# Row blocks in the middle of the next tile's products, and products in couples on halves of TensorE's rows

## The reference, cut to what matters

```python
Kf = jnp.einsum('bjd,ed->bje', F, K_w)
S = jnp.einsum('bid,bjd->bij', F, Kf)
out = jnp.einsum('bij,ijd->bid', S, W)
out = out + jnp.einsum('bid,ed->bie', F, Q_w)
```

## Time and profile before

| what | value |
|---|---|
| median of three runs | 606.97 us |
| the profiled execution | 606.42 us |
| its span, first to last instruction | 604.6 us |
| TensorE busy (matmuls) | 596.4 us, 99% |
| VectorE busy | 399.2 us, 66% |
| ScalarE busy | 401.5 us, 66% |
| mean granted clock of TensorE | 0.998 of full speed |

### The profile page before, as it was taken

The page is one execution under the profiler, slowest core; times in us unless marked ns, Lnnn a source line. Parts: engine busy times, 40 slices in busy tenths (PEclk is TensorE's granted clock), DMA queues, the critical chain, the costliest instruction groups (busy, mean ns, idle before and its releaser), DMA issues.

```text
span 604.6 us, 17904 instructions
## 1 busy us (share of the span) xinstructions
PE 596.4 (99%) x7690; PEld 526.3 (87%) x7690; DVE 399.2 (66%) x412; ACT 401.5 (66%) x696; POOL 0.2 (0%) x4
## 2 busy tenths in 40 slices
PE   9999999999999999999999999999999999999995
PEld 7888989889898898988989898898988989889895
DVE  6556768567685675947749475685756768567486
ACT  7888393874938659295692947939387493865920
POOL 0000000000000000000000000000000000000000
PEclk9999999999999999999999999999999999999999
DMA  8644847457575575755657566484754857557177
GB/s 338 262 141 160 330 165 282 183 185 305 191 281 172 210 266 208 279 196 210 242 192 287 203 238 249 143 319 174 277 209 173 318 179 284 173 209 273 70 281 279
DMA packets 29452, 138.12 MB, mean 228 GB/s; under 512 B 3264, under 2 KB 3776, under 8 KB 21312
## 3 DMA queue, kind: packets, MB, share of 16 engines
q1 hardware_dynamic: 20736, 75.83, 31.8%
q10 hardware_dynamic: 8640, 61.15, 28.4%
HBM read 69.86 MB, written 67.11 MB: 227 GB/s over the span
## 4 chain that ended last, share of the span: by engine, by line
PE 98%; DVE 1%; issue 1%; DVEq 0%
PE ps L509 20%; PE ps L447 20%; PE ps L449 19%; PE ps L448 19%; PE ps L541 18%; DVE o_sb L372 1%; PE ps L576 1%; DVEq L49 0%; DVE o_sb L382 0%; PE ps L467 0%; PE ps L465 0%; PE ps L469 0%; DVE f_hi L388 0%; DVEq L115 0%
## 5 line engine op out<-in xcount | busy, mean ns | idle before, releaser
L337 DVE TENSOR_TENSOR f_lo<-f_ring,f_hi 128x1024 fp32r<-128x1024 f32 x124 | 151.8, 1224 | 168.2 <-ACT f_hi L217 166.6
L231 ACT ACTIVATE q_out<-ps 128x512 f32<-128x512 f32 x256 | 156.9, 613 | 6.6 <-PE ps L449 0.2
L222 ACT ACTIVATE kf<-ps 128x512 f32<-128x512 f32 x256 | 155.8, 609 | 3.5
L372 DVE TENSOR_TENSOR o_sb<-ps,q_out 128x1024 f32<-128x1024 f32 x127 | 145.1, 1215 | 19.4 <-PE ps L541 19.3
L240 ACT ACTIVATE s_t<-ps 128x512 f32<-128x512 f32 x32 | 19.1, 598 | 175.8 <-PE ps L509 175.8
L509 PE MATMUL ps<-f_ring,kf 128*64 128x64 f32 x4096 | 123.5, 222 | 0.3 <-issue 0.3
L509 PEld LDWEIGHTS ps<-f_ring,kf 128*64 128x64 f32 x4096 | 121.1, 138 | 2.6 <-issue 0.8
L541 PEld LDWEIGHTS ps<-s_t,w_sb 64*128 64x128 f32 x2048 | 115.6, 188 | 5.6 <-issue 5.6
L541 PE MATMUL ps<-s_t,w_sb 64*128 64x128 f32 x2048 | 118.6, 274 | 0.0
L447 PE MATMUL ps<-f_hi,k_hi 128*128 128x512 f32 x255 | 101.0, 396 | 0.0
L447 PE MATMUL ps<-f_hi,q_hi 128*128 128x512 f32 x256 | 100.0, 391 | 0.0
(11 more groups left out here) (39 smaller groups left out, 160.3 us busy)
## 6 DMA issues: line engine op xcount, KB each, us to landing
out<-o_sb SPq DMA_DIRECT2D x127, 512.0 KB, 3.5
f_ring<-f_t ACTq DMA_DIRECT2D x58, 1024.0 KB, 4.8
f_ring<-f_t SPq DMA_DIRECT2D x4, 1024.0 KB, 10.6
f_ring<-f SPq DMA_DIRECT2D x8, 256.0 KB, 5.3
w_sb<-w SPq DMA_DIRECT2D x1, 2048.0 KB, 17.8
out<-o_sb SPq DMA_DIRECT2D x2, 256.0 KB, 2.6
o_sb<-first SPq DMA_DIRECT2D x1, 192.0 KB, 2.9
o_sb<-first ACTq DMA_DIRECT2D x1, 192.0 KB, 3.4
```

The source lines that it names most:

```text
L222: nc.scalar.activation(kf[:, c // 2, c % 2 * CK:(c % 2 + 1) * CK, :, :].rearrange("d k h i -> d (k h i)"), ps[:, 2 * c % 8, :], COPY).then ...
L231: nc.scalar.activation(q_out[:, t % 2, :, :].rearrange("d i (h b) -> d i h b", h=2)[:, :, :, at:at + CK], q_bank(t * CHUNKS + c).rearrange ...
L337: nc.vector.tensor_tensor(f_lo[:, v % SPLIT, :], f_unit(v), f_hi[:, v % SPLIT, :].bitcast(F32), ALU.subtract).then_inc(flo_done, 1)
L372: nc.vector.tensor_tensor(o_sb[:, n % OBUF, :, :, :].rearrange("d x s b -> d s x b"), ps[:, bank:bank + 2, :].rearrange("d s (x b) -> d s ...
```

## The change

- The row blocks of tile t no longer follow the products of tile t+1; they stand in their middle, after the products of chunk 7 (MID = 8). The scores of tile t+1 follow the products of chunk 15 directly.
- From tile 1 on, a chunk's two products (each three matmuls of 128 rows) are cut at row 64 into six couples. `first_halves` issues three couples: the Q product on rows 0 to 63 beside the K product on rows 64 to 127. `second_halves` issues the other three: the K product on rows 0 to 63 beside the Q product on rows 64 to 127, added to the same banks. The second halves of a chunk come after the first halves of the next one, and wait for their own first halves (`half_done`). So TensorE's order is, with f and s for first and second halves: f0 f1 s0 f2 s1 f3 s2 f4 s3 f5 s4 f6 s5 f7 s6 s7, row blocks 0 to 7 of the tile before, f8 f9 s8 f10 s9 f11 s10 f12 s11 f13 s12 f14 s13 f15 s14 s15, then the scores.
- VectorE adds the row blocks between `both_f(v + 6)` and `low_f(v + 7)`.
- Waits follow: the first four row blocks wait for the copies of chunks 4 to 7, f8 to f11 wait for the sums of blocks 4 to 7, the scores wait for the copies of the last chunks, and the splits wait for `k_done` as well as `q_done`.
- The waits on `zeros_done` between products (FILL) are gone.

```diff
-FILL = {1: 0, 2: 56}
-FILL.update((t, 108) for t in range(3, TILES - 1))
-FILL[TILES - 1] = 132
+MID = 8
...
                 both_f(v + 4)
                 low_f(v + 5)
                 both_f(v + 6)
+                for k in range(UNITS):
+                    sum_out(t, k)
                 low_f(v + 7)
                 both_f(v + 8)
                 low_f(v + 9)
-                for k in range(UNITS):
-                    sum_out(t, k)
...
+            def products(step):
+                if step < TILES * CHUNKS - LATE:
+                    return (q_of(step), q_done), (k_of(step), k_done)
+                return (k_of(step), k_done), (k_of(step + 1), k_done)
...
+            def passes(dst, w_hi, w_lo, c, rows, first):
+                hi = f_hi[rows, c // 2 % SPLIT, piece_cols(c)]
+                lo = f_lo[rows, c // 2 % SPLIT, piece_cols(c)]
+                yield nc.tensor.matmul(dst, w_hi[rows, :], hi, start=first, stop=False)
+                yield nc.tensor.matmul(dst, w_hi[rows, :], lo, start=False, stop=False)
+                yield nc.tensor.matmul(dst, w_lo[rows, :], hi, start=False, stop=not first)
+
+            def first_halves(step):
+                (a, _), (b, _) = products(step)
+                for ins_a, ins_b in zip(passes(*a, lower, True), passes(*b, upper, True)):
+                    pass
+                ins_a.then_inc(half_done, 1)
+                ins_b.then_inc(half_done, 1)
+
+            def second_halves(step):
+
+                pe.wait_ge(half_done, 2 * (step - CHUNKS + 1))
+                (a, a_sem), (b, b_sem) = products(step)
+                for ins_b, ins_a in zip(passes(*b, lower, False), passes(*a, upper, False)):
+                    pass
+                ins_b.then_inc(b_sem, 1)
+                ins_a.then_inc(a_sem, 1)
...
-                    elif e % 2 == 0:
-
-
-                        pe.wait_ge(out_done, (t - 1) * UNITS + 5 + e // 2)
+
+                    pe.wait_ge(kf_copied, t * CHUNKS + max(2 * e + 2, 13 + e // 2))
+                    if e % 2:
+                        pe.wait_ge(q_copied, min(t * CHUNKS + 13 + e // 2, TILES * CHUNKS - LATE))
...
-                        pe.wait_ge(kf_copied, (t + 1) * CHUNKS + 13 + k)
-                        pe.wait_ge(q_copied, min((t + 1) * CHUNKS + 13 + k, TILES * CHUNKS - LATE))
+                        pe.wait_ge(kf_copied, (t + 1) * CHUNKS + MID - 3 + k)
+                        pe.wait_ge(q_copied, (t + 1) * CHUNKS + MID - 3 + k)
...
+                    if t >= 1 and MID <= c < MID + 4:
+
+                        pe.wait_ge(out_done, (t - 1) * UNITS + 5 + c - MID)
...
+                    first_halves(n)
+
+                    if c >= 1 and c != MID:
+                        second_halves(n - 1)
+                    if c == MID - 1:
+                        second_halves(n)
+                        rows_tile(t - 1)
+                if t >= 1:
+                    second_halves(min((t + 1) * CHUNKS - 1, TILES * CHUNKS - LATE))
...
             for t in range(TILES):
                 scores_tile(t)
                 if t < TILES - 1:
+
                     project(t + 1)
-                rows_tile(t)
+            rows_tile(TILES - 1)
```

More of the change, by code:

```diff
@@ L97, in build @@
         fhi_done, flo_done = sem("fhi_done"), sem("flo_done")
+        half_done = sem("half_done")
         k_done, kf_copied = sem("k_done"), sem("kf_copied")
@@ L208, in split_first @@
                 wait(act, q_done, 2 * (c // 2 - SPLIT) + 2)
+                wait(act, k_done, 2 * (c // 2 - SPLIT) + 2)
                 nc.scalar.activation(f_hi[:, c // 2 % SPLIT, piece_cols(c)], f_cols(c), COPY).then_inc(fhi_first, 1)
@@ L216, in split_f @@
                 act.wait_ge(q_done, 2 * (v - SPLIT) + 2)
+                act.wait_ge(k_done, 2 * (v - SPLIT) + 2)
                 nc.scalar.activation(f_hi[:, v % SPLIT, :], f_unit(v), COPY).then_inc(fhi_done, 1)
             def copy_kf(t, c):
-                act.wait_ge(k_done, t * CHUNKS + c + 1)
+                n = t * CHUNKS + c
+                act.wait_ge(k_done, n + 1 if n < TILES * CHUNKS - LATE else TILES * CHUNKS)
                 nc.scalar.activation(kf[:, c // 2, c % 2 * CK:(c % 2 + 1) * CK, :, :].rearrange("d k h i -> d (k h i)"),
@@ L225, in copy_q @@
             def copy_q(t, c):
-                act.wait_ge(q_done, t * CHUNKS + c + 1)
+                n = t * CHUNKS + c
+                act.wait_ge(q_done, n + 1 if n < TILES * CHUNKS - LATE else TILES * CHUNKS)
                 if c == 0:
@@ L328, in both_first @@
                 wait(dve, q_done, 2 * (c // 2 - SPLIT) + 2)
+                wait(dve, k_done, 2 * (c // 2 - SPLIT) + 2)
                 if c == 4:
@@ L350, in both_f @@
                 dve.wait_ge(q_done, 2 * (v - SPLIT) + 2)
+                dve.wait_ge(k_done, 2 * (v - SPLIT) + 2)
                 nc.vector.tensor_copy(f_hi[:, v % SPLIT, :], f_unit(v)).then_inc(fhi_dve, 1)
@@ L449, in three, with k_of, q_of @@
                 return nc.tensor.matmul(dst, w_lo[:, :], hi, start=False, stop=True)
+            def products(step):
+                if step < TILES * CHUNKS - LATE:
+                    return (q_of(step), q_done), (k_of(step), k_done)
+                return (k_of(step), k_done), (k_of(step + 1), k_done)
+            def k_of(c):
+                return ps[:, 2 * c % 8, :], k_hi, k_lo, c
+            def q_of(c):
+                return q_bank(c), q_hi, q_lo, c
+            def passes(dst, w_hi, w_lo, c, rows, first):
[17 more added lines that the diff above has]
+                ins_a.then_inc(a_sem, 1)
             def k_product(c):
@@ L470, in k_halves @@
                 ins.then_inc(k_done, 1)
[L472 to L498, removed]
             def scores(t, e):
@@ L514, in scores_tile @@
                 for e in range(UNITS):
[L515 to L522, removed]
-                    elif e % 2 == 0:
-                        pe.wait_ge(out_done, (t - 1) * UNITS + 5 + e // 2)
+                    pe.wait_ge(kf_copied, t * CHUNKS + max(2 * e + 2, 13 + e // 2))
+                    if e % 2:
+                        pe.wait_ge(q_copied, min(t * CHUNKS + 13 + e // 2, TILES * CHUNKS - LATE))
+                    if t == 0 and e == 0:
+                        for c in range(2):
+                            pe.wait_ge(f_first[c], 16)
                     scores(t, e)
@@ L571, in rows_tile, with project @@
                     row_block(t, k)
+            def project(t):
+                for c in range(CHUNKS):
+                    n = t * CHUNKS + c
+                    if n == TILES * CHUNKS - 1:
+                        break
+                    if n == 0:
+                        k_halves()
+                        pe.wait_ge(qlo_done, 1)
+                        q_product(n)
+                        continue
+                    if n < PIECES:
+                        pe.wait_ge(flo_first, n + 2)
+                    elif n % 2 == 0:
+                        pe.wait_ge(flo_done, n // 2 - FIRST + 1)
+                    if t >= 1 and MID <= c < MID + 4:
+                        pe.wait_ge(out_done, (t - 1) * UNITS + 5 + c - MID)
+                    elif c >= 4:
+                        pe.wait_ge(kf_copied, n - 2 if n == TILES * CHUNKS - LATE else n - 3)
+                    elif t >= 1:
+                        pe.wait_ge(s_copied_act if c % 2 else s_copied, (t - 1) * 2 + c // 2 + 1)
+                    if t == 0:
+                        k_product(n)
+                        if c >= 4:
+                            pe.wait_ge(q_copied, n - 3)
+                        q_product(n)
+                        continue
+                    if (4 <= c < MID or c >= MID + 4) and n < TILES * CHUNKS - LATE:
+                        pe.wait_ge(q_copied, n - 3)
+                    first_halves(n)
[6 more added lines that the diff above has]
+                    second_halves(min((t + 1) * CHUNKS - 1, TILES * CHUNKS - LATE))
             pe.wait_ge(zeros_done, 1)
```

## The result

The changed kernel takes 642.9 us in the median, the kernel before 607.3 beside it: 1.058 times as long, 95% interval 1.055 to 1.060. The forecast was 633, with 620 to 646 as its range, and slower with 0.85. The profiled execution took 642.96 us with a span of 641.2, 36.6 more than the span before.

What follows compares the result with a forecast made beforehand. TensorE, busy 99% of the span, was taken to bound the kernel. 606.42 us plus 25.6 (+1.7 a tile, fifteen tiles) plus 1.5 for spent waits gave 633.5, stated as 633, range 620 to 646.

Steps and rivals of the forecast that it cites:

- The late sums: Row blocks in the middle: VectorE's first sum at 3.45 holds block 4 by 1.25 us; 2.66 us of waits a tile.
- What was covered: Waits for f_lo at f14 (covered by 0.4 us), ScalarE's copies, half_done and the scores' new waits would cost nothing.
- The couples: Products as couples on row halves: 218.5 ns each instead of 226.5, gaining 0.77 us a tile.
- the dear end: Products: the upper bound for a couple's interval, 226.5 ns, the same as today's full product.
- Couples over 225 ns: Products: a named sign that the forecast is wrong, against couples expected 218 to 219 ns apart.
- The boundaries: Couples to row blocks and back cost nothing (0 to 0.2 us each, hidden); scores to couples 0.15 plus 0.11.
- The spent waits: TensorE's queue: removing them may shift instruction fetches into hiccups, 0.1 us a tile, 1.5 us in all.
- The same waits, couples as slow as today's products: Rival on the products: couples at 226.5 ns, +2.4 us a tile, +36, 643 us; chance 0.20.
- Faster: Rival on VectorE's sums: in time, first by 2.2 or so, a tile 36.0 us, about 592; chance 0.09.
- no change: Rival on the sums: right behind block 0, at 1.2, still 1.13 each, 600 to 607 us; chance 0.06.
- the dear end of my bounds: Removing the spent waits: a fetch hiccup of 0.54 us in each tile, 8 us in all.

Runs made afterwards that it cites:

- e1: Changed kernel with VectorE adding the row blocks before both_f(v + 6) instead of behind it: 623.5 us, 1.027 of the kernel before.
- e8: Changed kernel with each sum adding one bank of its two, the rest of the output left cleared: 619.3 us, 1.021 of the kernel before.
- e2: Changed kernel with whole products on the full array again, row blocks still in the middle: 621.3 us, 1.024 of the kernel before.
- The probe: Kernel before with ten series of matmuls on zeros ahead of it: rounded operands with 512 columns start every 227 ns, a couple 227, 128 columns 112.
- e4: Kernel before without its spent waits, nothing else changed: 615.0 us, 1.012 of the kernel before.
- e7: Changed kernel with whole products on the full array and sums ahead of both_f(v + 6): 618.7 us, 1.019 of the kernel before.
- e10: Kernel before's order with products in couples and spent waits, a third ahead of first halves, the others ahead of second halves: 614.9 us, 1.012 of the kernel before.

## Why the prediction was right, and where it was off

- **The late sums: right**, and by the steps given. Split over at 0.27 (measured 0.19), first sum at 3.45 (3.34), block 4 at 4.83 (4.62), f9 at 10.48 (10.27). From block 4 on, half of the 0.2 is the first sum's 0.11. The other half is the exposed load: a record of line 551 starts with its load, and the 0.11 lies behind that start. `e1` takes the lateness away, `e8` the pace, `e2` a part of both, and each gives back what the schedule says but for 3 to 10 us, in which stores and changes of tiling show. The waits sit at four blocks, f8 and f9, as said (that at f8, 0.22 us, stands in the profile as "issue").
- **What was covered: right.** No wait for a `f_lo`, for `half_done` or for ScalarE's copies shows. The cover of f14 was thin: low_f(v+7) ends at 259.77, f14 starts at 260.36, 0.6 later where 0.4 was forecast. That of f12 was wide, since low_f(v+6) is over before the sums; only in `e1`, with low_f(v+6) moved behind them, does f12 wait.
- **The couples: wrong, the term that was mis-sized.** I took 218.5 ns from the row blocks as the nearest rows and gave the dear end, 226.5, 0.20. It is 226.7: 31 half stages of three couples at 8.2 ns more, less what the wait takes in, are 0.7 us a tile, 10 us in all, the whole distance from 633 to 643. "Couples over 225 ns" was one of the signs that I had named for being wrong, and it came; the time lay in the range only because that had been stretched to 646 for this rival. The row blocks were near in tiling and far in what sets their interval. The probe shows that their 5 ns have nothing to do with halves: float32 with 128 columns takes 112 on the full array as well, and so does a rounded matmul of 128 columns that streams 53.3. What they share is a load of 128 columns for each matmul. The Trainium skill, page "TensorE: Matmul & The Clock Gate", section "LDWEIGHTS (loading the stationary operand)", gives such a load as columns/1.2, 106.7 ns, whatever the rows; the trace agrees to 5 ns, and shows that two halves' loads run side by side. A floor under every instruction, whatever it loads, would look alike in the probe; against it stand the scores, with loads of 64 columns, whose couples start every 58 ns (line 509). The figure of the Trainium skill that I weighed (same page, section "Back-to-back issue gap"), 2.5 ns over the columns at 2.4 GHz, holds neither for rounded operands with 512 columns (13.3) nor for float32, unless each column is counted as two steps (then 2.6).
- **The boundaries: right.** Couples to row blocks cost nothing (0.23).
- **The spent waits: the sum right, the reason too small.** I priced them at 1.5 us, from "most tiles today show none", which is what they are there for. In the changed kernel scores are 7.62 in all tiles but the last, and the second halves of the products are about 1 us over their shortest in all tiles together: 0.5 in one tile with a stop for nothing that the profile shows, 0.4 in the two tiles whose sums wait for stores. In the order of before the same removal costs 8 us (`e4`), the dear end of my bounds.
- **A slip in the sum.** The terms give 633.5 for the profiled execution and so 634 for the median, not 633.
- **The rivals.** "The same waits, couples as slow as today's products", 643 at 0.20, is what happened. "Faster" and "no change" failed where they were said to: the first sum came 1.1 us too late for the one and 2.1 for the other. That mending the order brings the middle place level is not so either: `e7` had the sums in time and still took 618.7, and even its undisturbed tiles are 0.2 us longer than before.

## What to carry to other kernels

When work is moved on an engine that was full, lay out the queue of the engine that serves it, with zero at the moved step, and look for what now stands ahead of the answer; here it was three instructions (low_f(v+5), the cast and low_f(v+6)), the first of which waits for products that end just before. Take the price of a new form of instruction from rows that share what sets its interval (operand kind, columns per weight load), not from rows that merely share its shape. And work that does nothing, such as waits long spent, may hold the count of instructions: price its removal with a run of its own.

## What was not expected of the hardware

- Rounded operands (fp32r) cost 13.3 ns a matmul beyond their columns at 256 and at 512 columns; float32 with 512 columns costs 2.6 a record, with two steps counted for each column.
- Matmuls with a load of 128 columns each start every 112 ns even where they have only 53.3 to stream; two row halves do so at the same time.
- TensorE idles up to about 1 us when a packet of instructions starts at the wrong moment. In the order of before, where row blocks stand ahead of the scores, a start 0.5 to 1.5 us into the scores mostly costs nothing; behind products no place cost the scores anything, and with spent waits spread over a chunk (`e10`) the stop moved into the products.
- With loads and stores together the DMA engines are full at about 400 to 410 GB/s. Stores of 512 KB at every 1.13 us ask for more; whether eight sums in a row run into it differs from tile to tile (ten of fifteen in `e1`, two in the changed kernel, none before).
